# A unit's row buffer is reloaded after its transposes, and the list is cleared in sixteen pieces

## The chip, the cores and the metric

One core of a Trainium2 chip runs the whole program. The metric is device time in microseconds, the median of three runs. The engines are named as in the profile: PE is TensorE, PEld its weight loads, DVE is VectorE, ACT is ScalarE, POOL is GpSimd, SP is SyncE; a letter q behind a name is that engine's own queue, where it waits and issues DMAs.

## What is computed

A decoder layer with a layer norm after each part, on x of 32 batches x 128 positions x 128 features:

```python
x = _layernorm(x + attn(x))          # per position, 16 x 16 over heads, quantised weights and activations
x = _layernorm(x + xattn(ctx, x))    # 16 heads of 8, 128 queries x 128 keys, in each batch
# mixture of experts, E = 8, F = 512, two experts for each token:
top_v, top_i = jax.lax.top_k(logits, 2)
top_w = jax.nn.softmax(top_v, axis=-1)
router_w = jnp.sum(jax.nn.one_hot(top_i, n_exp) * top_w[..., None], axis=-2)
h = jax.nn.relu(jnp.einsum('bsd,efd->bsef', tgt, W1) + b1)
o = jnp.einsum('bsef,edf->bsed', h, W2) + b2
tgt2 = jnp.einsum('bsed,bse->bsd', o, router_w)
x = _layernorm(x + _layer_norm(tgt + tgt2, gamma, beta))
```

## The kernel before

**Stages.** Each engine has its program written out by hand; semaphores are the only link between them. The first loop (`a_turn`, to about 374 us) does the self-attention, four batches a turn (TB = 4, T = 8 turns and two more for the lag). The second (`b_turn`, about 374 to 700 us) does the cross-attention, four steps j in each turn u, one batch a step, and from turn 3 on also the routing: each token's row (128 features as f16 high and low parts, its id, its router weight) is written by POOL with indirect DMAs into the list `xs` in HBM, at a place that belongs to its expert (`post_rows`, L761). The third loop (about 700 to 916 us) runs over NU = 46 units of U = 256 rows, each of one expert; the rest is the last norm.

**Clearing the list.** A unit may hold fewer than 256 tokens, so `xs` (32,768 rows of 144 floats and 256 more, 18.9 MB) is first filled with rows of zeros whose id is 2**20. ACT issues these DMAs in the first turn of the second loop: four of 4.6 MB, one a step (L1383), and one of 144 KB (L1388), between its copies. `padded` counts them; POOL waits for all of them (`number_rows(0)`, turn 4, step 0) before it posts the first row.

**A unit.** SP loads the 256 rows of unit j into one of XD = 5 buffers, `xu[j % 5]` (L579). DVE takes the ids, min(id, an unused place), into `ids` (`keep_ids`, L1883); PE turns the rows over (`turn_over`, four transposes, L1132) into the one bank 7, DVE copies that to `xuT` (`turn_copy`, L1890). PE multiplies up (12 matmuls, L1144 to L1146), ACT and DVE split the result (L1403, L1895), PE multiplies down (26 matmuls, L1157 to L1163), ACT scales it by the router weight, which it reads from column D + 1 of `xu[j % 5]` (`unit_out`, L1412), and POOL scatters it to `ys` in two indirect DMAs (`send`, L809). PE's order in iteration j is up(j), turn_over(j + 2), down(j - 1); DVE's is h_low(j), keep_ids(j + 2), turn_copy(j + 2); ACT's is h_high(j), unit_out(j - 1). ou has OD = 3 buffers, so unit_out(j) waits until unit j - 3 is sent.

**What lets a buffer go.** SP loads unit j when unit j - 5 has left `unit_out` (`ou_ready`), because ACT still reads its weight, and when its ids are taken. `keep_ids(j)` waits until unit j - 5 is sent, because POOL reads `ids[j % 5]`.

**Other work in the third loop.** In iterations 2 to 6 the last tile is routed; behind sends 5 to 12 POOL posts its eight parts (L761). SP's queue, in order: loads of units 0 to 28, a wait until units 20 to 22 are sent, eight DMAs of 256 KB that fetch finished rows (`load_rows`, L588), load of unit 29 and on. From iteration 28 on DVE, ACT and POOL also sum and norm the first four tiles.

The profile names a tensor by the allocation it lies in: xu is "Y", ou, h_hi, h_lo and xuT are "W_raw". Matmuls of the down product carry no shapes.

Of the kernel before, what the change touches and what calls it, by code (L numbers as in the profile page):

```python
# [8 lines left out]
def decoder_layer(nc, x, ctx_1024, mask, wq, wk, wv, wo, Wq, bq, Wk, bk, Wv, bv,  # L9
                  Wr, br, W1, b1, W2, b2, gamma, beta, out):  # L10
    F32, BF16, F16 = mybir.dt.float32, mybir.dt.bfloat16, mybir.dt.float16
    U8, U32, I32 = mybir.dt.uint8, mybir.dt.uint32, mybir.dt.int32
    ALU, ACT, AX = mybir.AluOpType, mybir.ActivationFunctionType, mybir.AxisListType

    B, P, D = x.shape
    H, HD = 16, D // 16
    E, F = W1.shape[0], W1.shape[1]
    FC = F // P
    TB = 4
# [16 lines left out]
    UNUSED = E * B * P  # L36
    RW = D + 16
    PR = 8
    XD, OD = 5, 3
    FIRST_FINAL = NUS[0] + 5  # L40
    PADS = TB + 1
    CREDIT = 16

    ctx = ExitStack()
    with ctx:
        def sb(name, shape, dt=F32):
            return ctx.enter_context(nc.sbuf_tensor(name, shape, dt))
# [16 lines left out]
        class Chain:  # L64
# [9 lines left out]
            def settle(self):  # L74
                self.eng.wait_ge(self.s, self.n + self.turn)
# [252 lines left out]
        in_use = sb("in_use", [P, NUS[0]])  # L328
        row_f = sb("row_f", [P, NUS[0]])
        unit_tab = sb("unit_tab", [P, 2, NU], I32)  # L330
        ids = sb("ids", [P, XD, 2], I32)
        unused_ids = sb("unused_ids", [P, NU, 2], I32)
        pad = sb("pad", [P, PR, RW])
        b2_rows = sb("b2_rows", [P, D], BF16)
# [2 lines left out]
        xs = nc.dram_tensor("xs", [E * B * P + U, RW], F32, kind="Internal").ap()  # L337
        ys = nc.dram_tensor("ys", [2 * B * P + NU * U, D], F32, kind="Internal").ap()
# [5 lines left out]
        xu = [old[:, n_staged + 2 * RW * n:n_staged + 2 * RW * (n + 1)].rearrange("p (s r) -> p s r", s=2) for n in range(XD)]  # L344
# [23 lines left out]
        padded = ctx.enter_context(nc.semaphore("padded"))  # L368
# [20 lines left out]
        ids_ready = ctx.enter_context(nc.semaphore("ids_ready"))  # L389
        t_psum = ctx.enter_context(nc.semaphore("t_psum"))  # L390
# [5 lines left out]
        ou_ready = ctx.enter_context(nc.semaphore("ou_ready"))  # L396
# [102 lines left out]
        def sent_by(eng, j):  # L499

            eng.wait_ge(sent[j % OD], 32 * (j // OD + 1))
# [25 lines left out]
        def _(sp):  # L527
# [45 lines left out]
            def load_unit(j):  # L573

                if j >= XD:
                    sp.wait_ge(ou_ready, j - XD + 1)
                    sp.wait_ge(ids_ready, j - XD + 1)
                row = sp.value_load(unit_tab[0:1, 0, j:j + 1], min_val=0, max_val=UNUSED)
                sp.dma_start(xu[j % XD], xs[bass.ds(row, U), :].rearrange("(s p) r -> p s r", p=P)).then_inc(unit_in[j % XD], 16)  # L579
# [47 lines left out]
        def _(pool):  # L627
# [118 lines left out]
            def number_rows(t):  # L746
# [9 lines left out]
                if t == 0:  # L756
                    pool.wait_ge(padded, 16 * PADS)

# [45 lines left out]
            def send(j):  # L804

                pool.wait_ge(ids_ready, j + 1)
                pool.wait_ge(ou_ready, j + 1)
                for s in range(2):
                    pool.indirect_dma_start(ys[:], bass.IndirectOffsetOnAxis(ap=ids[:, j % XD, s:s + 1].bitcast(U32), axis=0),  # L809
                                            ou[j % OD][:, s, :], None).then_inc(sent[j % OD], 16)  # L810

            def invert(t, ve, rstd, was_ready, ready):
# [385 lines left out]
        def _(act):  # L1198
# [130 lines left out]
            def b_turn(u, parity, there):  # L1329
                for j in range(TB):  # L1330
# [42 lines left out]
                    if j == 0 and there(0):  # L1373
# [2 lines left out]
                        act.copy(x1T[:].rearrange("p a d -> p (a d)"), PS[:, 4, :]).then_inc(x1T_ready, 1)  # L1376
                        after(act, cT_psum, u + 1)
                        act.copy(cT[:].rearrange("p a d -> p (a d)"), PS[:, 5, :]).then_inc(cT_ready, 1)
                    if u == 0:
                        if j == 0:  # L1380
                            act.wait_ge(pad_ready, 1)
                        blocks = E * B // PR // TB
                        act.dma_start(xs[P * PR * blocks * j:P * PR * blocks * (j + 1), :].rearrange(  # L1383
                            "(n p r) d -> p n (r d)", p=P, r=PR),
                            pad[:].rearrange("p r d -> p (r d)").unsqueeze(1).broadcast_to((P, blocks, PR * RW))
                            ).then_inc(padded, 16)
                        if j == TB - 1:
                            act.dma_start(xs[UNUSED:UNUSED + U, :].rearrange("(p r) d -> p (r d)", p=P),  # L1388
                                          pad[:, 0:U // P, :].rearrange("p r d -> p (r d)")).then_inc(padded, 16)
                    if route_turn(u) and j == 1:  # L1390
# [15 lines left out]
            def unit_out(j):  # L1406

                act.wait_ge(o_psum, j + 1)
                if j >= OD:
                    sent_by(act, j - OD)  # L1410
                for s in range(2):
                    last = act.activation(ou[j % OD][:, s, :], PS[:, 4 + j % 2, s * D:(s + 1) * D], ACT.Copy,  # L1412
                                          scale=xu[j % XD][:, s, D + 1:D + 2])
                last.then_inc(ou_ready, 1)

            def normalise(t):
# [16 lines left out]
            for j in range(NU):  # L1433
# [10 lines left out]
                t, n = divmod(j - FIRST_FINAL, 4)  # L1444
# [19 lines left out]
        def _(dve):  # L1464
            ch = Chain(dve, dve_chain)
            step, settle = ch, ch.settle
# [411 lines left out]
            def keep_ids(j):  # L1878

                dve.wait_ge(unit_in[j % XD], 16 * (j // XD + 1))  # L1880
                if j >= XD:
                    sent_by(dve, j - XD)
                dve.tensor_tensor(ids[:, j % XD, :], xu[j % XD][:, :, D].bitcast(I32), unused_ids[:, j, :], ALU.min  # L1883
                                  ).then_inc(ids_ready, 1)

            def turn_copy(j):
# [53 lines left out]
            for j in range(NU):  # L1940
# [11 lines left out]
                t, n = divmod(j - FIRST_FINAL, 4)  # L1952
# [50 lines left out]
```

## Time and profile before

| | us |
|---|---|
| median of 3 runs | 970.67 |
| lowest, highest | 961.45, 972.70 |
| the profiled execution | 966.13 |
| its span, first to last instruction | 964.3 |
| PE, DVE, POOL, ACT busy | 676.3, 680.9, 550.8, 413.1 |
| mean granted TensorE clock | 0.876 of full |

No engine is busy throughout: each share is a mean over stages that wait for different things. So the chain of waits, followed back from the last instruction, is what to read, stretch by stretch; the busy times tell only how much room an engine has. Of the time outside the span 1.8 us are left, 966.13 - 964.3.

### The profile page before, as it was taken

How to read it: one execution, taken by the hardware profiler on the slowest of the kernel's cores; microseconds unless marked ns; L12 is line 12 of the kernel's file. 1: busy time of each engine (PE TensorE's matmuls, PEld its weight loads, DVE VectorE, ACT ScalarE, POOL GpSimd, SP SyncE). 2: the span in 40 equal slices, each digit the busy share in tenths (PEclk: the TensorE clock that was granted, in tenths of full speed). 3: DMA queues.
4: the chain of work that ended last, by engine and by line, in shares of the span. 5: the costliest groups of instructions: out<-in, count | busy, mean ns of one | idle time of the engine just before them, and what ended most of it. 6: DMA issues, size and time to landing. Idle time of an engine off the chain costs nothing.

```text
span 964.3 us, 20612 instructions
## 1 busy us (share of the span) xinstructions
PE 676.3 (70%) x6882; PEld 599.8 (62%) x6882; DVE 680.9 (71%) x1781; ACT 413.1 (43%) x933; POOL 550.8 (57%) x624
## 2 busy tenths in 40 slices
PE   1427686786876843389999999988678788688700
PEld 1326686776776842268888888876557667666600
DVE  4969999999999953356797787786246344467554
ACT  2412223223223314167776776755334244355523
POOL 5245566776776724255567777763355644466642
PEclk9769989799799775589999999989879999899955
DMA  6401111111111114950000000010012222423231
GB/s 209 87 6 12 12 17 12 17 16 12 16 16 13 14 28 183 421 209 13 13 5 31 29 20 31 20 45 20 24 49 67 74 72 69 140 68 85 68 93 44
DMA packets 114870, 57.41 MB, mean 60 GB/s; under 512 B 70752, under 2 KB 105248, under 8 KB 114784
## 3 DMA queue, kind: packets, MB, share of 16 engines
q1 hardware_dynamic: 105488, 26.49, 12.5%
q10 hardware_dynamic: 4304, 19.02, 4.8%
q0 software_dynamic: 4992, 10.76, 3.3%
q8 instruction: 53, 0.87, 0.4%
q14 instruction: 33, 0.27, 0.1%
HBM read 22.29 MB, written 33.96 MB: 58 GB/s over the span
## 4 chain that ended last, share of the span: by engine, by line
PE 33%; DVE 30%; issue 17%; ACT 6%; POOL 3%; DMA 2%; another core or an unknown queue 2%; ACTq 2%; SPq 1%; DVEq 1%; POOLq 0%
PE PS L1078 10%; DVE S L1619 5%; PE PS L994 4%; PE PS L903 3%; PE PS L1004 3%; DVE QKT L480 2%; DVE QK L472 2%; PE PS L1047 2%; DVE bn L1591 2%; DVE yq L1693 2%; PE PS L1163 2%; DVE W_raw L1895 1%; PE PS L1161 1%; PE PS L1046 1%
## 5 line engine op out<-in xcount | busy, mean ns | idle before, releaser
L903 PE MATMUL PS<-QKT,ident 128*128 128x128 f32 x1024 | 134.0, 294 | 12.2 <-POOL QKT L480 10.7
L809 POOL DMA_INDIRECT ys<-W_raw,ids x92 | 90.0, 978 | 89.7 <-ACT W_raw L1412 65.5
L903 PEld LDWEIGHTS PS<-QKT,ident 128*128 128x128 f32 x1024 | 130.2, 209 | 17.0 <-issue 10.9
L480 POOL TENSOR_TENSOR QKT<-E,qkv 128x1408 f32<-128x1408 f32 x32 | 104.1, 3254 | 54.0 <-ACT E L1237 53.6
L1078 PE MATMUL PS<-W_raw 128*72 128x128 f32 x1024 | 128.5, 280 | 7.5 <-DVE att L1839 4.8
L1078 PEld LDWEIGHTS PS<-W_raw 128*72 128x72 f32 x1024 | 114.8, 146 | 13.1 <-issue 5.6
L1818 DVE TENSOR_REDUCE m<-PS 128x8 f32<-128x1024 f32 x64 | 78.0, 1219 | 56.4 <-PE PS L1004 56.4
L1895 DVE SCALAR_TENSOR_TENSOR W_raw<-PS,W_raw 128x512 f16<-128x512 f32 x92 | 60.3, 687 | 80.8 <-ACT W_raw L1403 54.2
L472 POOL TENSOR_TENSOR QK<-qkv 128x1408 f32<-128x1408 f32 x32 | 84.4, 2636 | 56.7 <-ACT qkv L1274 49.6
L925 PE MATMUL PS<-QK,ident 128*128 128x128 f32 x512 | 77.6, 315 | 47.9 <-DVE S1d L1627 26.3
L925 PEld LDWEIGHTS PS<-QK,ident 128*128 128x128 f32 x512 | 72.6, 226 | 50.4 <-issue 28.4
L761 POOL DMA_INDIRECT xs<-Y,spot_u x64 | 63.7, 995 | 21.9 <-issue 15.0
L1162 PE MATMUL PS<-W_hi,W_raw 128*128 x368 | 74.9, 227 | 1.1 <-issue 1.1
L1161 PE MATMUL PS<-W_hi,W_raw 128*128 x368 | 74.9, 227 | 1.2 <-issue 1.1
L1163 PE MATMUL PS<-W_lo,W_raw 128*128 x368 | 74.8, 227 | 1.0 <-issue 1.0
L784 POOL TENSOR_TENSOR qk_rest<-qk_f,QK 128x128 f32<-128x128 f32 x64 | 26.0, 428 | 86.3 <-ACT QK L1341 86.1
L994 PE MATMUL PS<-ident,QK 128*128 128x128 bf16 x768 | 57.1, 227 | 21.1 <-ACT QKT L1346 15.0
L1353 ACT ACTIVATE W_raw<-PS 128x1024 f32<-128x1024 f32 x64 | 65.8, 1028 | 12.4 <-remote 9.7
L792 POOL TENSOR_SCALAR QK<-qk_rest 128x128 bf16<-128x128 f32 x128 | 67.9, 553 | 0.0
L1412 ACT ACTIVATE W_raw<-PS,Y 128x128 f32<-128x128 f32 x92 | 28.8, 365 | 88.6 <-PE PS L1163 51.2
L994 PEld LDWEIGHTS PS<-ident,QK 128*128 128x128 bf16 x768 | 50.3, 102 | 24.1 <-ACT QKT L1346 15.3
L1619 DVE TENSOR_REDUCE S<-QK 128x128 f32<-128x1024 f32 x32 | 61.8, 1930 | 3.6 <-POOL QK L472 3.6
(270 smaller groups left out, 1683.7 us busy)
## 6 DMA issues: line engine op xcount, KB each, us to landing
xs<-pad ACTq DMA_DIRECT2D x4, 4608.0 KB, 23.5
Y<-xs SPq DMA_DIRECT2D x46, 144.0 KB
W_raw<-ys SPq DMA_DIRECT2D x16, 256.0 KB
W_raw<-in_L_ffn_W_dram SPq DMA_DIRECT2D x1, 2048.0 KB
shuffle<-hctx SPq DMA_DIRECT2D x32, 64.0 KB, 3.0
Y<-shuffle SPq DMA_DIRECT2D x32, 64.0 KB, 1.8
cs<-in_ctx_dram SPq DMA_DIRECT2D x8, 256.0 KB, 2.9
out_dram<-W_raw SPq DMA_DIRECT2D x8, 256.0 KB, 2.3
```

What stands on the lines that cost most here:

```text
L472: return eng.tensor_tensor(prod1[:, i % 2, :].rearrange("p (d h t) -> p d h t", d=HD, h=H)[:, :, first:end, :], q.broadcast_to((P, HD, n, ...
L480: return eng.tensor_tensor(prod2[:, i % 2, :].rearrange("p (t h d) -> p t h d", t=H, h=H)[:, :, first:end, :], a.broadcast_to((P, H, n, HD ...
L809: pool.indirect_dma_start(ys[:], bass.IndirectOffsetOnAxis(ap=ids[:, j % XD, s:s + 1].bitcast(U32), axis=0), ou[j % OD][:, s, :], None).th ...
L903: last = pe.matmul(PS[:, 6, 0:D], ident[:], prod2[:, i % 2, D * t:D * (t + 1)], start=(t == 0), stop=(t == H - 1))
L925: last = pe.matmul(PS[:, 7, 0:D], ident[:], prod1[:, i % 2, H * H * d:H * H * d + D], start=(d == 0), stop=(d == HD - 1))
L994: last = pe.transpose(PS[:, bank, g * 64:(g + 1) * 64].bitcast(BF16), QK[:, j, side, HR * g:HR * g + HR, :].rearrange("p h r -> p (h r)"), ...
L1078: last = pe.matmul(PS[0:HO, 7, a * P:(a + 1) * P], v_frame[:, i % 2, a, HO * n:HO * (n + 1)], PT[:, i % 2, 8 * a + n, :], start=(n == 0), ...
L1161: pe.matmul(o, h_hi[j % 2][:, c, tokens], w_hi, start=False, stop=False)
L1162: pe.matmul(o, h_lo[j % 2][:, c, tokens], w_hi, start=False, stop=False)
L1163: last = pe.matmul(o, h_hi[j % 2][:, c, tokens], w_lo, start=False, stop=(c == FC - 1))
L1619: step(dve.tensor_reduce(S1[:], prod1[:, i2 % 2, :].rearrange("p (d a) -> p a d", d=HD)[:, D:2 * D, :], AX.X, ALU.add))
L1818: dve.tensor_reduce(half_heads(m2[:], a), banks(a).rearrange("p r (g t) -> p r g t", t=P), AX.X, ALU.max).then_inc(max_done, 1)
```

## The change

The list is cleared by sixteen DMAs of 1.18 MB, one in each step of turns 0 to 3, with the 144 KB one behind the first; `padded` has to reach 17 where it was 5. The router weight of each row is copied by DVE into an own table `w_rows` of eight entries in `keep_ids`, with a wait for that copy ahead of the ids; `unit_out` scales by the table and waits for `ids_ready`. `ids` has eight entries too, so `keep_ids(j)` waits for the send of unit j - 8. SP loads unit j when the transposes of unit j - 5 are done (`t_psum`) and its ids are taken.

```diff
--- before.py
+++ after.py
@@ -36,9 +36,9 @@
     UNUSED = E * B * P
     RW = D + 16
     PR = 8
-    XD, OD = 5, 3
+    XD, OD, KD = 5, 3, 8
     FIRST_FINAL = NUS[0] + 5
-    PADS = TB + 1
+    PADS = 4 * TB + 1
     CREDIT = 16
 
     ctx = ExitStack()
@@ -328,7 +328,8 @@
         in_use = sb("in_use", [P, NUS[0]])
         row_f = sb("row_f", [P, NUS[0]])
         unit_tab = sb("unit_tab", [P, 2, NU], I32)
-        ids = sb("ids", [P, XD, 2], I32)
+        ids = sb("ids", [P, KD, 2], I32)
+        w_rows = sb("w_rows", [P, KD, 2])
         unused_ids = sb("unused_ids", [P, NU, 2], I32)
         pad = sb("pad", [P, PR, RW])
         b2_rows = sb("b2_rows", [P, D], BF16)
@@ -573,7 +574,7 @@
             def load_unit(j):
 
                 if j >= XD:
-                    sp.wait_ge(ou_ready, j - XD + 1)
+                    sp.wait_ge(t_psum, j - XD + 1)
                     sp.wait_ge(ids_ready, j - XD + 1)
                 row = sp.value_load(unit_tab[0:1, 0, j:j + 1], min_val=0, max_val=UNUSED)
                 sp.dma_start(xu[j % XD], xs[bass.ds(row, U), :].rearrange("(s p) r -> p s r", p=P)).then_inc(unit_in[j % XD], 16)
@@ -806,7 +807,7 @@
                 pool.wait_ge(ids_ready, j + 1)
                 pool.wait_ge(ou_ready, j + 1)
                 for s in range(2):
-                    pool.indirect_dma_start(ys[:], bass.IndirectOffsetOnAxis(ap=ids[:, j % XD, s:s + 1].bitcast(U32), axis=0),
+                    pool.indirect_dma_start(ys[:], bass.IndirectOffsetOnAxis(ap=ids[:, j % KD, s:s + 1].bitcast(U32), axis=0),
                                             ou[j % OD][:, s, :], None).then_inc(sent[j % OD], 16)
 
             def invert(t, ve, rstd, was_ready, ready):
@@ -1376,15 +1377,14 @@
                         act.copy(x1T[:].rearrange("p a d -> p (a d)"), PS[:, 4, :]).then_inc(x1T_ready, 1)
                         after(act, cT_psum, u + 1)
                         act.copy(cT[:].rearrange("p a d -> p (a d)"), PS[:, 5, :]).then_inc(cT_ready, 1)
-                    if u == 0:
-                        if j == 0:
+                    if u < 4:
+                        if u == 0 and j == 0:
                             act.wait_ge(pad_ready, 1)
-                        blocks = E * B // PR // TB
-                        act.dma_start(xs[P * PR * blocks * j:P * PR * blocks * (j + 1), :].rearrange(
-                            "(n p r) d -> p n (r d)", p=P, r=PR),
-                            pad[:].rearrange("p r d -> p (r d)").unsqueeze(1).broadcast_to((P, blocks, PR * RW))
-                            ).then_inc(padded, 16)
-                        if j == TB - 1:
+                        n = TB * u + j
+                        act.dma_start(xs[P * PR * 2 * n:P * PR * 2 * (n + 1), :].rearrange("(n p r) d -> p n (r d)", p=P, r=PR),
+                                      pad[:].rearrange("p r d -> p (r d)").unsqueeze(1).broadcast_to((P, 2, PR * RW))
+                                      ).then_inc(padded, 16)
+                        if n == 0:
                             act.dma_start(xs[UNUSED:UNUSED + U, :].rearrange("(p r) d -> p (r d)", p=P),
                                           pad[:, 0:U // P, :].rearrange("p r d -> p (r d)")).then_inc(padded, 16)
                     if route_turn(u) and j == 1:
@@ -1406,11 +1406,12 @@
             def unit_out(j):
 
                 act.wait_ge(o_psum, j + 1)
+                act.wait_ge(ids_ready, j + 1)
                 if j >= OD:
                     sent_by(act, j - OD)
                 for s in range(2):
                     last = act.activation(ou[j % OD][:, s, :], PS[:, 4 + j % 2, s * D:(s + 1) * D], ACT.Copy,
-                                          scale=xu[j % XD][:, s, D + 1:D + 2])
+                                          scale=w_rows[:, j % KD, s:s + 1])
                 last.then_inc(ou_ready, 1)
 
             def normalise(t):
@@ -1878,9 +1879,11 @@
             def keep_ids(j):
 
                 dve.wait_ge(unit_in[j % XD], 16 * (j // XD + 1))
-                if j >= XD:
-                    sent_by(dve, j - XD)
-                dve.tensor_tensor(ids[:, j % XD, :], xu[j % XD][:, :, D].bitcast(I32), unused_ids[:, j, :], ALU.min
+                if j >= KD:
+                    sent_by(dve, j - KD)
+                step(dve.tensor_copy(w_rows[:, j % KD, :], xu[j % XD][:, :, D + 1]))
+                settle()
+                dve.tensor_tensor(ids[:, j % KD, :], xu[j % XD][:, :, D].bitcast(I32), unused_ids[:, j, :], ALU.min
                                   ).then_inc(ids_ready, 1)
 
             def turn_copy(j):
```

## Rows read from the trace of the kernel before

**Rows 1.** Chain of waits, 360 to 520 us: start us, us, what.

```profile
391.64 1.01 ACT QKT L1361
392.65 4.94 ACTq L1383
397.63 10.92 ACTq L1388
...
409.06 0.51 ACT QK L1341
...
426.95 0.45 PE PS L994 x8
```

**Rows 2.** Line L1383 alone: duration ns min/median/max; us to landing.

```profile
L1383 ACTq DMA_DIRECT2D xs<-pad x4: 378/404/5946, 374.6 to 391.6; - x4
...
DMA to landing us min/median/max: 13.1/23.5/30.0
```

**Rows 3.** Timeline of TensorE, 372 to 425 us: start, us, line, [idle before].

```profile
395.11 1.80 PE L994 MATMUL PS<-ident,QK 128*128 128x128 bf16 x16
410.53 1.03 PE L994 MATMUL PS<-ident,QK 128*128 128x128 bf16 x8 [13.62 <-ACT QKT L1346]
```

**Rows 4.** Windows: length, busy PE PEld DVE ACT POOL, clock, DMA share, GB/s.

```profile
409.00:414.00 5.00, 2.28 (x14) 2.05 (x15) 0.00 (x0) 2.60 (x5) 3.82 (x9) 0.50 1.03 424
430.00:460.00 30.00, 29.18 (x370) 25.96 (x364) 21.44 (x56) 20.90 (x33) 15.32 (x36) 1.00 0.04 11
```

**Rows 5.** Timeline of ScalarE, 492 to 516 us.

```profile
501.13 1.65 ACT L1302 ACTIVATE X<-yq_f,shift,rstd 128x128 f32<-128x128 f32 x4
```

**Rows 6.** Timeline of GpSimd, 484 to 530 us.

```profile
503.48 1.31 POOL L761 DMA_INDIRECT xs<-Y,spot_u  x1 [0.91 <-POOL Y L752]
...
514.74 0.81 POOL L784 TENSOR_TENSOR qk_rest<-qk_f,QK 128x128 f32<-128x128 f32 x2 [2.19 <-ACT QK L1341]
```

**Rows 7.** Waits, 640 to 905 us: us in total, times, longest us.

```profile
ACT W_raw L1412 <- remote: 34.7, 10, 6.8
...
PE PS L1132 <- DVE W_raw L1890: 18.4, 13, 6.0
...
PE PS L1132 <- DMA Y<-xs: 11.0, 8, 5.6
...
DVE ids L1883 <- DMA ys<-W_raw,ids: 5.5, 4, 2.3
```

**Rows 8.** Chain of waits, 735 to 830 us.

```profile
755.88 0.37 ACT W_raw L1412
...
756.98 2.11 DMA Y<-xs
...
818.30 0.40 SPq L588
...
826.45 3.89 DMA Y<-xs
```

**Rows 9.** Timeline of GpSimd, 733 to 770 us.

```profile
746.96 0.97 POOL L809 DMA_INDIRECT ys<-W_raw,ids  x1 [2.25 <-ACT W_raw L1412]
...
753.32 0.97 POOL L761 DMA_INDIRECT xs<-Y,spot_u  x1 [0.30 <-issue]
756.99 0.97 POOL L809 DMA_INDIRECT ys<-W_raw,ids  x1 [2.71 <-ACT W_raw L1412]
```

**Rows 10.** Windows of L1144 alone, four matmuls a unit: busy us (count).

```profile
737.00:775.00 38.00, 7.96 (x29) 2.84 (x29) 0.96 0.25 74
775.00:822.00 47.00, 13.74 (x47) 4.89 (x47) 0.93 0.28 80
```

**Rows 11.** Line L1883 alone: duration ns min/median/max.

```profile
L1883 DVE TENSOR_TENSOR ids<-Y,unused_ids x46: 146/152/1866, 702.6 to 904.3; 128x2 int32<-128x2 int32 x46
```

**Rows 12.** Timeline of VectorE, 733 to 770 us.

```profile
734.72 0.17 DVE L1783 SCALAR_TENSOR_TENSOR units<-run_first,units 128x8 f32<-128x8 f32 x1
734.92 0.17 DVE L1785 TENSOR_TENSOR_SCAN ends<-ones,units 128x8 f32<-128x8 f32 x1
```

## The prediction

> **What bounds the kernel now.** I read the chain of waits first, because no engine is busy for more than 71% of the span. In the second loop's first turn the chain leaves the engines' work: ACT stands in its own queue for 4.94 us at L1383 and 10.92 us at L1388, from 392.65 to 408.55 [rows 1]. Those are DMA issues. An issue takes 0.38 to 0.40 us as long as the queue takes it, and 5.95 us for the fourth, when three DMAs of 4.7 MB are ahead of it [rows 2]. TensorE is idle for 13.62 us behind this [rows 3]. Once the second loop runs full, TensorE is its bound: busy 29.18 of 30 us from 430 to 460, at full clock [rows 4]. In the third loop it goes round: ACT's scaling of a unit (L1412), SP, the load of a later unit (2.11 us), its transposes [rows 8]. There the waits view says how much of that TensorE really stands for: 11.0 us in 8 waits for the loads, one of them 5.6 us; 18.4 us in 13 for DVE's copy of the transposes before; ACT waits 34.7 us in 10 for a product of TensorE that comes late [rows 7].
>
> **The padding, what it removes.** Sixteen pieces of 1.18 MB. The first turn now issues four of them and the 144 KB one, 4.9 MB in all, where the first two of before (9.4 MB) were taken in 0.4 us each [rows 2]: neither the 4.94 nor the 10.92 us is left. That is 15.9 us of ACT, but not all of it is gained, because other work lay in its shadow. ACT's next copy but one needs the transposes that TensorE ran from 395.11 for 1.80 us, sixteen of them; the first eight end near 396.0, the copy takes 1.0 us [rows 1, 3], so TensorE's eight transposes of 410.53 start near 397.1: 410.5 - 397.1 = 13.4 us gained. The clock adds to it. From 409 to 414 us the granted clock is 0.50, the lower level (1.2 GHz), behind that long idle stretch; eight transposes take 1.03 us there and 0.45 us later at full clock [rows 1, 3, 4]. Without the idle stretch the rise may come earlier. At best every TensorE piece of the chain from 410.5 to about 417 us, some 5 us of it, halves with its clock: 0 to 3 us. I take 1.7.
>
> **The padding, what it adds.** Twelve issues fall into turns 1 to 3, between ACT's copies, at 0.4 us [rows 2]. TensorE is the path there and ACT is busy 20.90 of 30 us, some 5.2 of a step of 7.5 [rows 4], so ten of them fit into its gaps. In turns 2 and 3, step 3, the piece stands in front of the norm of a tile (1.65 us, L1302) [rows 5], behind which TensorE waits for ACT: 2 x 0.4 = 0.8 us. All twelve on the path would be 4.8, none 0. The wait for `padded` moves: the last piece is issued in turn 3, step 3, just ahead of that norm at 501.1 (times as before, without the shift) [rows 5]. A whole DMA alone landed in 13.1 us [rows 2]; at 424 GB/s [rows 4] its 4.7 MB take 11.1, so 2.0 are fixed, and a quarter lands in 2.0 + 2.8 = 4.8 us, at 505.9. POOL's first post was at 503.48, of which 0.3 us is the restart: it stands for 2.6 us. Behind it on POOL's queue are that post, a second, and the splitting of the next batch (L784 and on), whose result TensorE transposes a step later; in the next step POOL itself waits 2.19 us for ACT [rows 6], so it makes good all but 0.5 us. 0 to 2.7. In sum: 13.4 + 1.7 - 0.8 - 0.5 = 13.8 us, from 5.9 (all costs, no clock) to 16.4.
>
> **The row buffer, what it removes.** Load j goes out when the transposes of unit j - 5 are done, in iteration j - 7, instead of in iteration j - 4; it is wanted in iteration j - 2. It takes 2.11 us plus SP's 0.7 between 755.88 and 756.98 [rows 8], and the distance is now five iterations of 4 us or more. So all of TensorE's waits for loads but one go: 11.0 - 5.6 = 5.4 us [rows 7]. The one stays: load 29 is behind `load_rows` on SP's queue, eight issues from 818.30 on, and goes out at 826.45 and lands 3.89 us later [rows 8]. `load_rows` waits for the sends of units 20 to 22, which the change does not touch, so it starts little earlier: 0 to 1, I take 0.6 us. Next, keep_ids no longer waits for the send of unit j - 5: 5.5 us in four waits of DVE [rows 7]. DVE has room in most iterations; I take 1 of 0 to 5.5.
>
> **The row buffer, what it adds.** One DVE operation a unit with a wait for it ahead of the ids. The trace has none such; the nearest are L1883 itself, the same 128 x 2 elements, median 0.152 us [rows 11], and two dependent small operations that start 0.20 us apart [rows 12]. So 0.20 us a unit, 46 x 0.20 = 9.2 us of DVE, at least 0.15. It costs where TensorE waits for the DVE operation behind it: 13 of 46 [rows 7], 13 x 0.20 = 2.6 us; elsewhere it lies in DVE's waits for ACT. ACT's added wait for `ids_ready` is passed iterations before. Net 5.4 + 0.6 + 1.0 - 2.6 = 4.4 us, from -9.2 (all on the path, no gain) to +12.
>
> **Sum.** 13.8 + 4.4 = 18.2. Against the profiled execution's 966.13 that is 947.9. The median of the three runs is 970.67, 4.5 higher, and on its scale it is 952.5. I say 951 for the median, nearer to the second. Its own range is 944 to 957. A difference of 2%, 19.4 us, is about what a measurement of this kernel can tell from no change; the runs of before lie within 1.2% of each other.
>
> **Rivals.**
>
> *Only the padding pays.* POOL's indirect DMAs come in rows without a gap, five pitches in 753.32 - 746.96 = 6.4 us, 1.27 each, and then a gap of 2.7 us; two such rows start 10.0 us apart, for two units [rows 9]. ACT's late products (34.7 us) [rows 7] end just behind such rows. If it is this cycle and not the load that paces the loop, the load gaps that go are taken up by it. Then the row buffer part gives between 0 and -2.6, the total is 11 to 14: about 955 to 959. For it: units pass at 7.25 in 38 us, 5.2 us each, in just this stretch, against 4.0 us in the next (47 matmuls of L1144, 11.75 units, in 47 us) [rows 10], and the chain goes through both. Against it: the 5.4 us are gaps of TensorE that end with the landing, seven of them.
>
> *The loop comes free.* If the load closes the cycle just named, the stretch of posts falls to POOL's own rate, three indirect DMAs a unit, 3 x 1.27 = 3.8 us: 7.25 x 1.4 = 10 us; and the next from 4.0 to 3.8: 2.4 us. Less 2.6 for the copy, 9.8 instead of 4.4: 23.6 in all, and with the clock's and the ids' upper ends 27. That is 939 to 947.
>
> *Slower: the copy waits for POOL.* The one mechanism on the other side. L1883 took 1.87 us at the most, where 0.15 is its median [rows 11], and nothing in the operation differs from the other 45; so DVE can be held from outside, by POOL as the likeliest. If the new copy, whose ends are both in SBUF, is held by each indirect DMA in flight (0.97 us) [rows 9], it costs up to 46 x 0.97 = 44.6 us: 948 + 45 = 993. At 18.2 / 46 = 0.40 us a copy the gain is gone, at 37.6 / 46 = 0.82 it is slower by 2%. Against it: L1883 has two SBUF inputs, ran 46 times beside two such DMAs a unit, and its median is still 0.152. By the Trainium skill, SBUF — State Buffer, section "SBUF: two separate sides", a fp32 copy from SBUF to SBUF on VectorE takes the port pair that it shares with GpSimd, and the descriptors of a GpSimd DMA can't be written meanwhile; by that rule the copies would hold up POOL's sends and be held by them. No row of before has such a copy beside a send, so the trace neither agrees nor disagrees.
>
> *The change doesn't do what it says.* The pieces might still block ACT. 4.9 MB in a turn that took 9.4 MB without a block speaks against it; 0.01.
>
> **Chances.** The forecast 0.50, only the padding 0.24, the loop comes free 0.20, the copy waits for POOL 0.05 (three quarters of it slower by 2%), the last 0.01. The range goes from the middle of the fast rival to beyond the padding alone, with the padding's own costs: 940 to 962. Faster by over 2%, under 951.3, is half of the forecast's 0.50 and nearly all of the fast rival: 0.44. Slower by over 2%: 0.04. Within 2%: 0.52.
>
> **What would show it.** In the new profile: L1383 sixteen times with a maximum near 0.4 us, no wait of ACT over 5 us before 420 us, DMA traffic of 150 to 200 GB/s over four turns in place of 424 over 50 us, TensorE dense from near 400 us. POOL's first post with a wait of 2 to 3 us for a DMA and no wait of TensorE behind it. In the third loop no wait of L1132 for the load of a unit but that of unit 29, near 5 us; L1883 without waits for sends; the new copy at 0.15 us, 46 times. I am wrong if TensorE's third loop keeps its time although the load waits are gone (first rival), if the second loop's first turn finds a new wait, of POOL or of the clock, or if the copy or the sends (0.96 us each) have grown.

## The result

The kernel before took 969.78 us in the runs beside the changed one (median of 4, 961.45 to 972.70), the changed kernel 956.1 us (median of 4, 953.78 to 959.08). The ratio is 0.9884, with a 95% interval of 0.9847 to 0.9920: some 11 us faster (8 to 15), an interval that also holds the 13.7 us between the two medians. The forecast was 951, its range 940 to 962. The time is that of the first rival, only the padding pays (955 to 959). The profiled execution took 957.23 us, its span is 955.5 us; of before these were 966.13 and 964.3. One execution of a kernel below, `e4_copy_3x`, took 1045.1 us at a granted clock of 0.634, and the ratios leave it out.

In what follows the lines of the changed kernel are one higher than those of before (L994 is L995), the same between the clearing and `unit_out` (L1403 stays), and three higher behind `keep_ids` (L1890 is L1893).

**The clearing.** The pieces' line alone (duration ns min/median/max; us to landing), which answers [rows 2]:

```profile
L1384 ACTq DMA_DIRECT2D xs<-pad x16: 378/379/452, 374.4 to 487.3; - x16
...
DMA to landing us min/median/max: 4.3/4.8/5.8
```

No issue takes longer than 0.45 us, and a piece lands in 4.8 us at the median, the value worked out beforehand. The same turn on TensorE (timeline: start, us, line, [idle before]), which answers [rows 3]:

```profile
395.79 0.98 PE L995 MATMUL PS<-ident,QK 128*128 128x128 bf16 x8
397.73 0.62 PE L995 MATMUL PS<-ident,QK 128*128 128x128 bf16 x8 [0.96 <-ACT QKT L1347]
```

The eight transposes that stood at 410.53 stand at 397.73; 13.62 us of idle time are 0.96. The granted clock behind them (windows: length, PE busy, clock, DMA share, GB/s):

```profile
400.00:405.00 5.00, 4.80 (x50) 0.66 0.59 212
405.00:410.00 5.00, 2.44 (x37) 1.00 0.64 242
410.00:415.00 5.00, 5.00 (x48) 0.66 0.19 76
415.00:420.00 5.00, 5.00 (x73) 1.00 0.59 236
```

0.66 over 5 us is 3.4 us at the lower level and 1.6 at the higher. The second such stretch, 410 to 415, comes behind a stretch in which TensorE worked for 2.44 of 5 us. That alone doesn't bring the fall: in `e7_no_posts`, a kernel below whose clearing is the same and whose keys' copy of batch 2 starts within 0.2 us of this one's, TensorE worked for 2.46 us there, and the clock stayed up:

```profile
405.00:410.00 5.00, 2.46 (x37) 1.00 0.61 233
410.00:415.00 5.00, 5.00 (x66) 1.00 0.19 78
```

Of the twelve profiles with small pieces eight show the second fall and four (`e3_turn_first`, `e5_act_copy`, `e7_no_posts`, `e10_after_again`) don't; what decides it no run here shows. GpSimd's first post (timeline), which answers [rows 6]:

```profile
490.28 0.16 POOL L753 IOTA Y<- 128x8 int32 x1
494.11 1.30 POOL L762 DMA_INDIRECT xs<-Y,spot_u  x1 [3.67 <-issue]
```

3.67 us of idle time where 0.91 stood: 2.76 us more, for the last piece. And the issue of that last piece among ScalarE's work (timeline):

```profile
486.99 1.01 ACT L1362 COPY QKT<-PS 128x1024 bf16<-128x1024 bf16 x1 [0.42 <-PE PS L995]
487.33 0.38 ACTq L1384 DMA_DIRECT2D xs<-pad  x1
487.89 1.03 ACT L1354 ACTIVATE W_raw<-PS 128x1024 f32<-128x1024 f32 x1
```

The issue (487.33 to 487.71) lies inside the copy that runs from 486.99 to 488.00, and the next activation starts without a gap.

**The third loop.** Waits, 629 to 896 us (us in total, times, longest us), which answer [rows 7]:

```profile
ACT W_raw L1413 <- remote: 29.3, 10, 6.1
...
PE PS L1133 <- DVE W_raw L1893: 21.0, 18, 6.2
...
PE PS L1133 <- DMA Y<-xs: 4.4, 1, 4.4
...
DVE w_rows L1884 <- DMA Y<-xs: 3.0, 1, 3.0
```

Of eight waits for loads (11.0 us) one is left, that of unit 29, and the waits of VectorE for sends (5.5 us) are gone. So the change does in the trace what it was to do. Yet the stretch with the load waits takes as long as before. L1145 alone (its four matmuls a unit: length, PE busy (count), PEld busy (count), clock, DMA share, GB/s), which answers [rows 10]:

```profile
726.00:766.00 40.00, 8.72 (x28) 3.02 (x28) 0.83 0.24 69
766.00:812.00 46.00, 13.15 (x48) 4.65 (x48) 1.00 0.29 82
```

Seven units in 40 us, where 7.25 took 38: 5.7 us each against 5.2, at a mean granted clock of 0.83 against 0.96. Which of the two, the slower units or the lower clock, brought the other isn't shown. The new copy, by its tile (duration ns min/median/max):

```profile
L1884 DVE COPY w_rows<-Y x46: 156/159/1973, 691.5 to 895.0; 128x2 f32<-128x2 f32 x46
```

**Where the time went.** Matching events of the two traces, the changed kernel's time less that of before: the transposed keys' copy (L1847 of the changed kernel) of batch 2, ahead of the stall, -0.2 us, of the two batches behind it -13.7, of batch 5 -12.1, and so to batch 14; first `turn_copy` of the third loop -10.9; that of unit 15 -6.4, of unit 24 -8.1, of unit 33 -11.8, of unit 45 -9.1; the last norms -8.8.

For the experiments I read two lengths from every trace, which leave out the 5 us by which the start of the second loop varies from execution to execution: the **second loop**, from the copy of the keys of batch 2 to the first `turn_copy`, and the **third loop**, from there to the first norm of the last tile. Before: 305.6 and 247.4. Changed: 294.9 and 249.5. So in these two traces the gain is in the second loop, 10.7 us, and the third gave back 2.1. The traces have a scatter of their own: with sixteen pieces the second loop takes 291.4 to 294.9 us on chips of this kind.

The experiments ran on four chips. On two of them the kernel before takes 967 and 971 us, as in the first comparison ("the first kind" below), on two 924 us ("the second kind"), whose third loop is some 25 us shorter and whose second some 16. Ratios are always to the kernel before on the same chip, and lengths are compared within one kind.

### The profile page after: what moved, and what is told of

Its sections match the earlier page's. It is cut to its first block, busy times and chain, and to the rows that moved or that the text cites. A ratio compares the mean times of both kernels' runs of the same rounds, so it can differ in the third digit from the quotient of the medians.

```text
span 955.5 us, 20670 instructions
## 1 busy us (share of the span) xinstructions
PE 680.5 (71%) x6882; PEld 603.8 (63%) x6882; DVE 691.5 (72%) x1827; ACT 413.1 (43%) x933; POOL 550.1 (58%) x624
## 4 chain that ended last, share of the span: by engine, by line
DVE 35%; PE 33%; issue 16%; ACT 5%; POOL 4%; DMA 3%; SPq 1%; DVEq 1%; another core or an unknown queue 1%; ACTq 0%; POOLq 0%
PE PS L1079 9%; DVE S L1620 5%; PE PS L995 3%; PE PS L904 3%; PE PS L1005 3%; DVE W_raw L1898 2%; DVE QKT L481 2%; DVE QK L473 2%; DVE bn L1592 2%; PE PS L1048 2%; PE PS L1164 2%; DVE yq L1694 2%; PE PS L1162 1%; PE PS L1047 1%; PE PS L1163 1%
## 5 line engine op out<-in xcount | busy, mean ns | idle before, releaser
L904 PEld LDWEIGHTS PS<-QKT,ident 128*128 128x128 f32 x1024 | 130.3, 209 | 17.1 <-issue 11.0
L1079 PE MATMUL PS<-W_raw 128*72 128x128 f32 x1024 | 132.1, 285 | 9.3 <-DVE att L1840 4.8
L1079 PEld LDWEIGHTS PS<-W_raw 128*72 128x72 f32 x1024 | 118.0, 149 | 15.4 <-issue 9.0
L762 POOL DMA_INDIRECT xs<-Y,spot_u x64 | 63.7, 995 | 25.9 <-issue 19.1
L1403 ACT ACTIVATE W_raw<-PS 128x512 f16<-128x512 f32 x92 | 51.5, 596 | 30.0 <-remote 15.3
L1238 ACT ACTIVATE E<-S1d,c_qk 128x256 f32<-128x256 f32 x32 | 16.3, 508 | 108.8 <-DVE S1d L1628 108.8
L1413 ACT ACTIVATE W_raw<-PS,w_rows 128x128 f32<-128x128 f32 x92 | 28.7, 363 | 79.3 <-PE PS L1164 47.8
```

The source lines that it names most:

```text
L904: last = pe.matmul(PS[:, 6, 0:D], ident[:], prod2[:, i % 2, D * t:D * (t + 1)], start=(t == 0), stop=(t == H - 1))
L1079: last = pe.matmul(PS[0:HO, 7, a * P:(a + 1) * P], v_frame[:, i % 2, a, HO * n:HO * (n + 1)], PT[:, i % 2, 8 * a + n, :], start=(n == 0), ...
```

## Experiments

### The two parts apart

`e1_pad_only` is the kernel before with the sixteen pieces alone; `e2_rows_only` is the changed kernel with the clearing of before, whose diff is the same, read backwards:

```diff
-                    if u == 0:
-                        if j == 0:
+                    if u < 4:
+                        if u == 0 and j == 0:
                             act.wait_ge(pad_ready, 1)
-                        blocks = E * B // PR // TB
...
+                        n = TB * u + j
```

> The kernel before with only the sixteen pieces. Theory A (the clearing pays by itself, as the prediction's first part has it, and the row buffer's part comes to nothing): the unit loop starts 11 us sooner, as in the trace after, and keeps it, so the time is 11 us below before, ratio 0.988 to 0.989, the same as the whole change. Theory B (the row buffer's part also pays its 4.4 us): this kernel gives only 7 to 8 us, ratio about 0.992. Theory C (the row buffer's part costs the 2 us that the loop lost between the traces): 13 us below before, ratio about 0.986, and faster than the whole change.

> The whole change with the clearing in four big pieces again, so only the row buffer's part differs from before. Theory A: the waits of the matmuls on loads (11.0 us) are gone, but the time comes back as other waits, ratio 0.999 to 1.001. Theory B: -4.4 us, ratio 0.995. Theory C: +2 us, ratio 1.002. In every case the schedule up to the unit loop is that of before within 0.3 us.

Measured, both on one chip of the first kind: the clearing alone 953.14 us against 967.1, ratio 0.9858 (0.9830 to 0.9885), 13.7 us faster by the ratio; the row buffer's part alone 969.92, ratio 1.0025 (1.0004 to 1.0045), 2.4 us slower (0.4 to 4.4). Together -11.3, and the whole change had 0.9884, -11.2. Theory C came out by the middle values: the clearing is worth more than the whole change shows, and the row buffer's part costs what the third loop lost. The intervals of the clearing alone and of the whole change overlap, so it is the 1.0025, whose interval leaves out 1, and the third loops that carry this.

In the trace of the second the stall is back as it was, only a little longer (chain of waits):

```profile
391.27 5.91 ACTq L1384
397.21 11.19 ACTq L1389
```

That the schedule up to the third loop would be that of before within 0.3 us didn't hold: batch 5 comes 2.8 us later in it, 1.3 of them by the longer stall, the rest in a stretch with 23.9 us at the lower clock against 17.1, and the second loop is 4.2 us longer. The row buffer's part touches nothing there, so of the 2.4 us between the medians only what the third loop shows, 2.0, is put down to it.

The second loop took 305.6 and 309.8 us with the four big pieces (before, `e2_rows_only`) and 292.0, 294.9, 291.4 and 292.7 with sixteen (`e1_pad_only`, the changed kernel and the two runs of the next part). The third took 248.2 us in `e1_pad_only` and 249.4 in `e2_rows_only`, against 247.4 of before.

### What the copy costs

```diff
+                step(dve.tensor_copy(w_rows[:, j % KD, :], xu[j % XD][:, :, D + 1]))
+                settle()
+                step(dve.tensor_copy(w_rows[:, j % KD, :], xu[j % XD][:, :, D + 1]))
+                settle()
                 dve.tensor_tensor(ids[:, j % KD, :], ...
```

> The whole change with the copy of the two weights and its settling done three times, 0.4 us more per unit. If the copy lies on the path in 13 to 18 units, 5.2 to 7.2 us slower than the whole change; if in all 48 units, 19 us slower; if it is hidden, no difference.

```diff
-                    keep_ids(j + 2)
                     turn_copy(j + 2)
+                    keep_ids(j + 2)
```

> The whole change, but VectorE copies the turned rows (turn_copy) ahead of the copy of the weights and the ids (keep_ids). If the 0.20 us copy lies on the path in the units that wait for VectorE (units 30 to 45, where the loop lost 2.7 us), those units get 13 to 18 times 0.2 us back and, as the min (146 ns) moves behind too, up to another 2 us: ratio 0.995 to 0.997 of the whole change's time, 0.984 of before. If the copy is hidden and another thing cost the loss, no difference from the whole change (0.9985 to 1.0015 of it).

Measured beside the two above: three copies 964.04 us, ratio 0.9961 (0.9939 to 0.9983); the other order 956.16, ratio 0.9877 (0.9847 to 0.9908), which is the whole change's. Two more copies cost 7.9 us between these two medians, and 9.0 us in the third loop (258.5 against 249.5), above the 5.2 to 7.2 expected. That is 4.0 to 4.5 us for one copy, if the first costs what the second and third do, or 20 to 22 units in which its 0.20 us is on the path: more than the 13 of the prediction, fewer than 46.

The trace shows where. From about unit 32 on the starts of `turn_copy` repeat every four units. Of the changed kernel (timeline of VectorE):

```profile
853.30 0.42 DVE L1893 COPY W_raw<-PS 128x512 f16<-128x512 f16 x1
...
857.47 0.42 DVE L1893 COPY W_raw<-PS 128x512 f16<-128x512 f16 x1
...
862.20 0.42 DVE L1893 COPY W_raw<-PS 128x512 f16<-128x512 f16 x1
...
867.99 0.42 DVE L1893 COPY W_raw<-PS 128x512 f16<-128x512 f16 x1
```

The intervals are 4.17, 4.73 and 5.79 us. In the trace of before the same three are 3.96, 4.52 and 5.59; with three copies they are 4.58, 5.20 and 6.19. Each copy adds 0.20 to 0.23 us to each unit there. The chain of waits goes through VectorE's list (the halves of h, the copy, the ids, the turned rows, the sums of the finished tiles), and in two of the four units through ScalarE's norm of a finished tile between. The order of the list matters little: four units take 18.9 us in the changed kernel, 18.5 in `e3_turn_first` and 18.0 in before, so turning first gives back 0.3 of the 0.9 us. Its third loop takes 248.6 us, 0.9 less than the changed kernel's; the medians don't show it.

### The copy on another engine

```diff
+            def keep_weights(j):
+
+                act.wait_ge(unit_in[j % XD], 16 * (j // XD + 1))
+                act.copy(w_rows[:, j % KD, :], xu[j % XD][:, :, D + 1]).then_inc(w_kept, 1)
```

VectorE's copy is gone. ScalarE calls its own one unit ahead, behind its two halves of h; SP waits for `w_kept` too before it reloads a buffer, and `unit_out` waits for it in place of `ids_ready`.

> The whole change, but ScalarE copies the two weights (one unit ahead, with a semaphore of its own), so VectorE has the work of before. Theory D (the copy costs its 0.2 us in each unit in which VectorE sets the period, about 16 to 20 units, and the earlier reloading gives back 1 to 2 us): the time falls 3 to 5 us below the whole change, to a ratio of 0.984 to 0.9855 of before, 1 to 2 us better than the clearing alone; the repeated intervals of 4.2, 4.2, 4.8, 5.8 us between the copies of turned rows become 4.0, 4.0, 4.5, 5.6 again. Rival (ScalarE's copy delays the unit outputs by as much): no gain over the whole change, ratio 0.988.

This ran on a chip of the second kind, so I repeated it there beside the whole change and the clearing alone:

> The whole change with the two weights copied by ScalarE. VectorE's copy sets the period of some 16 units by 0.2 us each, so this is 2.5 to 4 us below the whole change (ratio 0.984 to 0.986) on either kind of chip; below the clearing alone by 0.5 to 1.5 us if the earlier reloading is worth something, level with it if not. Rival: the copy on ScalarE delays the unit outputs where these are waited for, and the time is that of the whole change.

> The whole change, beside the other two: ratio 0.988 to before, as measured first; the copies of turned rows at 4.2, 4.2, 4.8, 5.8 us from each other in units 33 to 45.

> The kernel before with only the sixteen pieces, beside the two below on one chip. If the row buffer's part costs 2 us, this is 0.002 below the whole change's ratio to before (0.986 against 0.988). On a chip on which a unit takes 3.1 to 3.3 us between units 10 and 28 (as in the last three traces), the loads land 2.2 us after their issue, and the row buffer's part could be worth more or less than that.

| on a chip of the second kind | median us | ratio, interval | third loop us |
|---|---|---|---|
| `e5_act_copy` (another chip) | 910.99 | 0.9861 (0.9837 to 0.9886) | 219.6 |
| `e11_act_copy_again` | 910.14 | 0.9845 (0.9814 to 0.9876) | 219.7 |
| `e10_after_again` | 913.08 | 0.9880 (0.9849 to 0.9911) | 224.2 |
| `e9_pad_only_again` | 914.12 | 0.9886 (0.9851 to 0.9921) | 221.8 |

Without VectorE's copy the third loop is 4.5 us shorter, the same 4.5 as above, and the median 2.9 us lower (`e11_act_copy_again` against `e10_after_again`, on one chip). The ratio of `e5_act_copy` is a little above the expected 0.984 to 0.9855, that of `e11_act_copy_again` within it. The period is that of before again, 3.95, 3.95, 4.52, 5.58 (timeline of VectorE, `e11_act_copy_again`):

```profile
807.01 0.41 DVE L1902 COPY W_raw<-PS 128x512 f16<-128x512 f16 x1
...
810.96 0.42 DVE L1902 COPY W_raw<-PS 128x512 f16<-128x512 f16 x1
...
814.91 0.42 DVE L1902 COPY W_raw<-PS 128x512 f16<-128x512 f16 x1
...
819.43 0.42 DVE L1902 COPY W_raw<-PS 128x512 f16<-128x512 f16 x1
...
825.01 0.41 DVE L1902 COPY W_raw<-PS 128x512 f16<-128x512 f16 x1
```

The whole change and the clearing alone can't be told apart here by their medians (1.0 us, the whole change the faster, against what was expected); their third loops differ by 2.4 us in the sense of the first kind. Against the clearing alone `e11_act_copy_again` is 4.0 us faster by the medians, where 0.5 to 1.5 was expected, and 2.1 by the third loop.

These traces also show that the earlier reloading does save time before something else takes it back. The clearing alone (waits, 660 to 855 us):

```profile
DVE ids L1882 <- DMA ys<-W_raw,ids: 10.1, 7, 3.1
...
PE PS L1132 <- DMA Y<-xs: 5.6, 2, 5.0
```

None of the 10.1 us is there in `e11_act_copy_again`, and units 12 to 18 take 19.1 us instead of 23.3. Its lead over the clearing alone, counted from the start of the loop, is 4.8 us at unit 18, 4.5 at unit 24, 3.0 at unit 30, 2.2 at unit 36 and 2.1 at the end. Between units 24 and 30 lies the load of unit 29 (chain of waits, `e10_after_again`):

```profile
756.44 0.97 POOL ys L810
...
757.71 2.27 DMA ys<-W_raw,ids
760.06 0.38 SPq L589
...
767.79 4.74 DMA Y<-xs
772.58 0.61 PE PS L1133 x4
```

Load 29 stands on SP's queue behind the eight row loads, and these behind the last send of unit 22, which goes through every engine of the loop. From 760.06 SP issues for 7.7 us, then the load lands 4.7 us later. The waits of TensorE for it are 5.0 us in the clearing alone, 6.5 in the whole change and 7.5 in `e11_act_copy_again`: the 2.5 us more are nearly all that its lead loses from unit 28 (5.4 us) to unit 29 (2.8). Where the remaining 0.8 us between units 30 and 36 went I did not find.

### Is it the earlier reload or the tables?

```diff
-                    sp.wait_ge(t_psum, j - XD + 1)
+                    sp.wait_ge(ou_ready, j - XD + 1)
```

> The whole change with its table and copy, but a reload again waits for the unit's output (ou_ready), as before. If the earlier reloading is worth the 1 to 2 us of theory D, this is 1 to 2 us slower than the whole change, ratio about 0.990, with 8 to 13 us of matmul waits on loads back. If it is worth nothing, no difference (0.988). If it costs (more transfers at once), faster than the whole change (0.986).

On the second kind, beside `e5_act_copy`: 913.66 us, ratio 0.9880 (0.9857 to 0.9903), the whole change's; third loop 224.88 us against its 224.24. TensorE's waits for loads (waits, 660 to 855 us, `e10_after_again` and then `e6_late_load`):

```profile
PE PS L1133 <- DMA Y<-xs: 6.5, 1, 6.5
```

```profile
PE PS L1133 <- DMA Y<-xs: 9.4, 3, 7.6
```

The longest of either is unit 29's. So only 2.9 us came back, where 8 to 13 were expected, and the loop got 0.6 us longer. On this kind the late reload costs little to begin with, and the run says nothing of the 11.0 us of the first kind. There the evidence is `e12_eight_pieces`, whose third loop is as long as that of before without the load waits. What the tables brought on the second kind beyond the copy's price is, by what is left (10.1 us of VectorE's waits are gone), `keep_ids` no longer waiting for sends.

### Does GpSimd's queue set the pace?

```diff
                 if 5 <= j < 5 + 2 * TB:
-                    post_rows(T - 1, (j - 5) // 2, (j - 5) % 2)
```

`e8_posts_as_copies` has two copies of 128 x 512 in the place of each post. In both the last tile's rows are not posted, and SP reads the finished rows of the tile before in their place, so these times are of a kernel that routes seven tiles of eight.

> The whole change without the last tile's eight posts in the unit loop; the last tile's rows are not routed and its outputs are read from another tile's rows, so part of the result is left out. If GpSimd's rows of indirect transfers set the pace of units 7 to 15 (the period there is 5.7 us against 4.3 before and behind), the stretch falls by 8 to 10 us and the end by as much, unless the last loads then wait. If they are only busy beside the path, the end moves by less than 2 us.

> As the run without the posts, but each of the eight posts replaced by two copies of a 128 x 512 tile on GpSimd (its queue is held about as long, with no transfer). If it is the time on GpSimd that holds the loop, this is as slow as the whole change (within 2 us) and 8 to 10 us slower than the run without posts. If it is the transfers, it is as fast as the run without posts.

Measured: 911.7 us, ratio 0.9869 (0.9838 to 0.9901), third loop 222.7; with the copies 915.25, ratio 0.9896 (0.9860 to 0.9932), third loop 224.6. Against the changed kernel's 224.2 that is 1.5 us less and 0.4 more. But they ran on a chip of the second kind, where the slow stretch that I wanted to explain is not there: units pass at 3.1 to 3.2 us from unit 12 to 28 with all posts in place. For that kind the answer is that the posts cost 1.5 us by the traces; the intervals of the ratios overlap. For the first kind the question is open.

### Half the pieces

```diff
-                    if u < 4:
+                    if u < 2:
...
-                        act.dma_start(xs[P * PR * 2 * n:P * PR * 2 * (n + 1), :]
+                        act.dma_start(xs[P * PR * 4 * n:P * PR * 4 * (n + 1), :]
```

`PADS` is 2 * TB + 1. The rest is the kernel of `e5_act_copy`, with the weights copied by ScalarE, so against the changed kernel two things differ: the second loop tells of the pieces, the third of the copy.

> The kernel of e5_act_copy and e11_act_copy_again (the weights copied by ScalarE), with the clearing in eight pieces of 2304 KB over two turns in place of sixteen of 1152 KB over four. At the 424 GB/s of the four big pieces one of 2.36 MB takes 5.6 us, and ScalarE comes to the next after 4 to 10 us (7.5 on average), so no more than two are ever outstanding. If the stall of before was the queue's filling (three pieces of 4.7 MB, each 11.1 us), ScalarE's issues take 0.4 to 0.5 us here too, the schedule of the first turns is that of the sixteen pieces, GpSimd's wait for the clearing (2.8 us) is gone, and as that wait was on no path, the time is that of the sixteen pieces within 1.5 us (ratio 0.983 to 0.987). If a single big piece is enough to hold ScalarE or the other transfers, some issues take 2 us and more and 2 to 6 us of the gain are lost (ratio 0.988 to 0.992).

It ran on a chip of the first kind: 953.12 us against 970.67, ratio 0.9835 (0.9789 to 0.9882), the lowest ratio of all, with an interval that holds those of the others. Its pieces (their line alone, then windows: length, busy PE PEld DVE ACT POOL, clock, DMA share, GB/s):

```profile
L1386 ACTq DMA_DIRECT2D xs<-pad x8: 378/379/452, 373.1 to 421.8; - x8
...
DMA to landing us min/median/max: 7.6/9.3/9.9
```

```profile
374.00:400.00 26.00, 16.17 (x120) 12.46 (x122) 11.33 (x25) 9.62 (x17) 15.92 (x37) 0.57 0.94 374
400.00:425.00 25.00, 22.08 (x266) 18.75 (x261) 15.60 (x34) 15.64 (x24) 12.03 (x28) 0.89 0.83 333
```

The DMA engines are nearly as loaded as in the kernel before (0.94 and 0.83 of their time, against 0.98 and 0.90 in the same windows), and ScalarE doesn't wait: the copies of the keys across the place of the old stall lie 13.5 us earlier than in before, as with sixteen. So the stall was no contention for DMA bandwidth. It was ScalarE's own queue. In before the first piece lands at 387.7, so at the fourth issue (391.65) two whole pieces of 4.7 MB are outstanding, not three, and that issue and the next are held at the rate at which they drain. Here one whole piece at most is outstanding when the next is issued. Whether the bytes or the number of pieces fill the queue isn't shown. GpSimd's first post no longer waits for the clearing (0.90 us of idle time), and the second loop is as long as with sixteen (294.8 us against 294.9). Counted from batch 2, the keys' copies lie 12.0 us earlier than in before at batch 14 and 12.0 at batch 20 here, 12.0 and 12.1 in the changed kernel, whose post did wait: that wait had cost nothing. The third loop takes 247.3 us, that of before.

## Why the prediction came out as it did

The time was in the range and 5 us above the forecast. The clearing's part was right in its sum, the row buffer's part had the wrong sign. The range held because it was drawn to take in the clearing alone, not because the mechanism forecast for the row buffer worked.

*The stall* was to give 13.4 us at the start of TensorE's eight transposes; they moved by 12.8, of which 0.2 were there before (410.53 to 397.73). The term missed ScalarE's two casts (L1341, L1342), which end at 396.8 and stand ahead of the copy that the transposes wait for. That other work lay in the shadow of ScalarE's 15.9 us was right; it is 3.1 us of it, not 2.5.

*The clock* was to add 1.7. It first added 0.9, so that the keys' copy behind the stall lies 13.7 us earlier: nearly all of it in two pieces of the chain that had run at the lower clock and now ran at the higher, the eight transposes (1.03 us, now 0.62) and the four that follow. Timelines of TensorE, before and then changed:

```profile
412.76 1.09 PE L1110 MATMUL PS<-ident,x1s 128*128 128x128 f32 x4 [1.19 <-ACT QKT L1361]
```

```profile
399.54 0.71 PE L1111 MATMUL PS<-ident,x1s 128*128 128x128 f32 x4 [1.19 <-ACT QKT L1362]
```

Then it took 1.6 (from -13.7 to -12.1). The step that failed is "Without the idle stretch the rise may come earlier. At best ..." with its 0 to 3 us: the rise came earlier, but the sum had no second fall, and the clock fell once more, for 3.4 us between 410 and 415, under work that ran at full clock before. In the profile of `e10_after_again` and three others the second fall is missing, and the lag of `e10_after_again`, counted from batch 2, stays at 13.6. So the clock's term is -0.7 us with the second fall and 0.9 without, where I had 1.7.

*Twelve more issues* were to cost 0.8 us. They cost nothing: the lag is -12.12 or -12.13 at every copy from batch 5 to 14. The step counted an issue as ScalarE's time. It is the sequencer's, and lies beside the operation that ScalarE runs.

*GpSimd's wait* was sized at 2.6 us and measured 2.76; its price was put at 0.5 and is nil within what the traces show (the lag goes from -12.13 at batch 14 to -12.32 at batch 16). Sum of the clearing: 13.8 forecast, 13.7 measured by the ratio on the first kind (11.1 to 16.4), 10.5 (7.3 to 13.8) on the second. By the lag it is 12.0 with the second fall and 13.5 to 13.7 without. So the agreement to 0.1 us is luck in part: 1.3 us of costs that weren't there stood in for what the stall and the clock gave less.

*The load waits* were to give 5.4 us, the ids 1.0, load 29 0.6. The waits went as forecast, all but one. The failed step is "all of TensorE's waits for loads but one go: 5.4 us": it took the waits for the path. On the first kind the loop without VectorE's copy takes 247.3 us (`e12_eight_pieces`) against 247.4 of before and 248.2 of the clearing alone, so 7.0 us of forecast gain were 0.1 to 0.9, in one trace of each; on the second kind 2.1. The counter-argument to the first rival, that those gaps of TensorE end with the landing, was no argument: take the landing away and the loop is as long. Of the 5.4 us only 2.5, in 2 waits, lay in the slow stretch of before (737 to 775 us); the changed kernel's is no faster without them, and what its units wait for instead is not found.

*The copy* was to cost 2.6 and costs 2.2 (247.3 in `e12_eight_pieces` to 249.5, first kind) to 4.5 us (both by two more copies and by taking it off VectorE). 0.20 us was right; the number of units, 13, was too small. It came from the waits of TensorE for VectorE, and in the last third of the loop every unit pays for the copy, not only those that such a wait is booked for.

*The rivals.* Only the padding pays was right, with the cycle named there doubtful: on chips of the second kind the same posts stand in the queue and the loop isn't held. The loop comes free would have been 3.8 us a unit in the stretch of posts; it is 5.7. The copy waits for POOL is excluded: of the 46 copies 16 run beside an indirect DMA of GpSimd, and their median is 159 ns, their longest 378. What does hold them is GpSimd's addition of beta. Timelines of VectorE and of GpSimd, changed kernel:

```profile
866.59 1.29 DVE L1884 COPY w_rows<-Y 128x2 f32<-128x2 f32 x1
```

```profile
866.60 1.25 POOL L821 TENSOR_TENSOR X<-X,bet 128x512 f32<-128x512 f32 x1
```

The copy ends 0.03 us after the addition; so do the two others that took over 1 us. In the kernel before it was the ids' operation, the 1.87 us that the prediction wondered about. Therefore the change adds nothing here: whichever comes first is held. The Trainium skill, SBUF — State Buffer, section "SBUF: two separate sides", says that VectorE and GpSimd lock a port pair against each other for a whole instruction; for operations of GpSimd the trace agrees, 3 times. Of its warning that such a copy starves GpSimd's DMAs nothing is to be seen with these 2 elements a partition: the sends stay at 0.96 us, and in `e10_after_again` the 22 that have a copy beside them land in 2.3 us at the median, the other 70 in 2.4.

## What to carry to other kernels

A wait that ends with a landing is not yet a gain: before pricing it, ask what the waiting engine would meet next, or delay and advance the landing by itself. An operation added to an engine whose list sets a period costs about its full length in every turn of it, and moving it within the list gave back only a third here, so put it on an engine that waits. And issue large transfers no faster than they drain: one of 2.4 MB a step held nobody, though it filled the DMA engines, where one of 4.7 MB a step stopped the engine that issued it.

## What was not expected of the hardware

**Chips differ.** Before takes 967 to 971 us on one kind of chip and 924 on the other, at nearly the same granted clock (the changed kernel 0.877 and 0.884 in its profiles). The changed kernel's second loop takes 294.9 us on the first and 276.2 on the second; the third loop takes 249.5 and 224.2. It isn't the length of the operations that I compared: `turn_copy` takes 0.41 to 0.42 us and a send 0.96 to 0.97 on both. On the first kind TensorE stands between matmuls of one unit with nothing to wait for (timeline, changed kernel):

```profile
742.98 0.27 PE L1147 MATMUL PS<-W_raw,W_lo 128*128 128x256 f16 x1 [1.05 <-issue]
...
743.72 0.27 PE L1145 MATMUL PS<-W_raw,W_hi 128*128 128x256 f16 x1 [0.47 <-issue]
...
744.44 0.28 PE L1146 MATMUL PS<-W_raw,W_hi 128*128 128x256 f16 x1 [0.45 <-issue]
...
745.86 0.37 PE L1147 MATMUL PS<-W_raw,W_lo 128*128 128x256 f16 x1 [1.14 <-issue]
```

and ScalarE waits 29.3 us for products that the trace can't place. Neither is there in `e10_after_again`. In the first trace these stands lie in a row of GpSimd's indirect DMAs (737.31 to 744.64) or up to 1.2 us behind it, which is why I tried to take the posts away; those runs fell on the other kind, and the cause stays open.

**An issue beside an operation.** ScalarE's DMA issue of 0.38 us runs while ScalarE copies. It costs the engine nothing, until its queue is full: then it held ScalarE for 5.0 and 10.9 us in the kernel before, and for 5.9 and 11.2 in `e2_rows_only`.
